# Gathers paced by the landing of the one three back, in a recommendation tower on one core

## What is computed

```python
e = stack([tbl_f[ids[:, f]] for f in range(26)], axis=1)      # (512, 26, 64): the gathers
x = layer_norm(dense_t @ Wd.T, gd, bd)                        # (512, 128)
y = layer_norm(einsum('bnd,ed->bne', e, Ws), gs, bs)          # (512, 26, 128)
y = layer_norm(einsum('bne,pn->bep', y, Wsi), gsi, bsi)       # mixes the 26 features to 32
T = concatenate([x[:, None, :], swapaxes(y, 1, 2)], axis=1)   # (512, 33, 128)
Z = einsum('bnd,bmd->bnm', T, T)                              # pair products of the 33
z = layer_norm(Z[:, TRIL_I, TRIL_J] @ Wl.T, gl, bl)           # 528 -> 512, 384 kept
h = concatenate([z, dense_t], axis=1)
h = relu(h @ W_top1 + b_top1); h = relu(h @ W_top2 + b_top2); out = h @ W_top3
```

## Time and profile before

| | us |
|---|---|
| median of 3 runs | 211.37 (209.83 to 212.67) |
| the profiled execution | 211.83 |
| its span, first to last instruction | 210.0 |

### The profile page before, as it was taken

How to read it: one execution, slowest core, us unless ns; L and a number is a source line. 1 busy time by engine, 2 the same in 40 slices (tenths; PEclk the granted TensorE clock), 3 DMA queues, 4 the chain that set the end, 5 groups by cost and what they waited for, 6 DMA issues and landing times.

```text
span 210.0 us, 4185 instructions
## 1 busy us (share of the span) xinstructions
PE 162.5 (77%) x1644; PEld 105.3 (50%) x1644; DVE 99.3 (47%) x192; ACT 88.5 (42%) x225; POOL 100.0 (48%) x113
## 2 busy tenths in 40 slices
PE   0593888683798795948986878579877969997996
PEld 0332635351355363726554637355555567465574
DVE  2463928635457655553072738260545574661011
ACT  2613235451164664541473436232644535642251
POOL 4777374667474664765546557736173710000000
PEclk9999589999599998596999999958999978999999
DMA  6713314172011144111101243101010630005100
GB/s 160 229 21 79 108 29 112 33 246 53 16 25 18 29 118 76 28 26 21 25 6 30 81 91 53 28 16 27 4 28 13 153 50 3 0 3 138 24 3 0
DMA packets 20260, 11.58 MB, mean 55 GB/s; under 512 B 12945, under 2 KB 17681, under 8 KB 20242
## 3 DMA queue, kind: packets, MB, share of 16 engines
q1 hardware_dynamic: 16226, 7.83, 14.2%
q0 software_dynamic: 3328, 3.41, 8.6%
q10 hardware_dynamic: 688, 0.08, 0.3%
HBM read 9.15 MB, written 2.16 MB: 54 GB/s over the span
## 4 chain that ended last, share of the span: by engine, by line
PE 63%; issue 19%; DVE 10%; DMA 4%; ACT 3%; SPq 0%; ACTq 0%; DVEq 0%
PE proj_ps L474 11%; PE mix_ps L440 10%; PE o_ps L490 8%; PE quad_ps L451 7%; PE dots_ps L465 6%; PE o_turn_ps L403 3%; PE o_turn_ps L528 2%; DVE var_p L881 2%; PE turn_ps L432 2%; PE o_ps L403 2%; DVE feats L905 2%; DVE e_prod L890 2%; DVE var_n L893 2%; PE o_ps L422 2%; PE dots_ps L396 2%
## 5 line engine op out<-in xcount | busy, mean ns | idle before, releaser
L373 POOL DMA_INDIRECT e_rows<-table_dram,rows_sb x104 | 99.1, 953 | 68.1 <-PE dots_ps L465 33.8
L890 DVE TENSOR_TENSOR e_prod<-quad_ps,e_rows 128x384 f32<-128x384 f32 (+1 forms) x16 | 9.5, 591 | 56.6 <-PE quad_ps L451 44.7
L465 PE MATMUL dots_ps<-feats 128*32 128x33 f32 x1024 | 19.1, 203 | 21.2 <-issue 20.8
L474 PE MATMUL proj_ps<-f_sb,proj_w 128*128 128x512 f32 x60 | 32.2, 619 | 1.3 <-DVE feats L905 0.6
L465 PEld LDWEIGHTS dots_ps<-feats 128*32 128x32 f32 x1024 | 14.6, 113 | 36.1 <-issue 35.0
L440 PE MATMUL mix_ps<-mixw_sb,e_unit 128*128 128x192 f32 (+4 forms) x128 | 26.7, 364 | 6.3 <-issue 5.1
L440 PEld LDWEIGHTS mix_ps<-mixw_sb,e_unit 128*128 128x128 f32 x128 | 24.8, 235 | 13.6 <-issue 9.9
L682 ACT COPY f_sb<-mix_ps 64x512 f32<-64x512 f32 x32 | 18.5, 579 | 20.1 <-PE mix_ps L440 16.4
L490 PE MATMUL o_ps<-wl_gained,z_pairs 128*128 128x512 f32 (+1 forms) x40 | 21.2, 664 | 0.5 <-DMA z_pairs<-z_dram 0.5
L451 PEld LDWEIGHTS quad_ps<-gram,e_cols 128*128 128x128 f32 x104 | 13.4, 194 | 16.3 <-issue 11.0
L881 DVE TENSOR_REDUCE var_p<-y_sq 128x16 f32<-128x512 f32 x32 | 20.5, 677 | 1.6 <-ACT y_sq L667 1.6
(11 more groups left out here) (142 smaller groups left out, 176.8 us busy)
## 6 DMA issues: line engine op xcount, KB each, us to landing
z_dram<-z_mine SPq DMA_DIRECT2D x4, 512.0 KB, 3.2
e_rows<-table_dram,rows_sb POOLq DMA_INDIRECT x104
w_sb<-w_dram SPq DMA_DIRECT2D x2, 512.0 KB
wl_sb<-wl_dram SPq DMA_DIRECT2D x2, 512.0 KB
w_sb<-w_dram SPq DMA_DIRECT2D x1, 768.0 KB
dense_sb<-dense_t_dram SPq DMA_DIRECT2D x1, 512.0 KB
wl_sb<-wl_dram SPq DMA_DIRECT2D x1, 256.0 KB
z_pairs<-z_dram SPq DMA_DIRECT2D x4, 64.0 KB, 2.1
```

The costliest lines, as they stand in the source:

```text
L373: pool.indirect_dma_start(out=e_rows[:, chunk, t, D * ab:D * (ab + 1)], out_offset=None, in_=table, in_offset=bass.IndirectOffsetOnAxis(ap ...
L465: mm = pe.matmul(dots_ps[PR * k:PR * (k + 1), (PR + 1) * g:(PR + 1) * (g + 1)], f[:, 2:PR + 2], f[:, 0:PR + 1], start=True, stop=True)
L474: pe.matmul(proj_of(s, ab), proj_w[:], f_sb[:, q % 2, ab, :], start=True, stop=True).then_inc(projected, 1)
L890: dve.tensor_tensor(e_prod[:, 0:2 * nt, :].rearrange("p a d -> p (a d)"), quad_ps[:, 0:P * nt], e_rows[:, chunk, t0:t0 + nt, :].rearrange( ...
```

## The change

The 16 semaphores of the slots are replaced by four, `landed[0]` to `landed[3]`; gather g adds to `landed[g % 4]`. Gather g waits for the landing of gather g - 3. The waits before slots 2 and 3 are gone; from slot 4 on a slot's first gather waits for `dots` of four slots back, as it did. Who reads a slot's landing (`turn`, SyncE's loads) waits on all four semaphores for their share of the gathers up to that slot's last (`rows_landed`). `variance_n` no longer waits for the landing; it waits for `quad`, which comes after `turn`.

```diff
--- before.py
+++ after.py
@@ -104,6 +104,14 @@
         if lo < hi:
             parts.append((t, lo - first_sample(t), lo - q * QB, hi - lo))
     return parts
+
+
+IN_FLIGHT = 3
+
+
+def gathers_up_to(s):
+
+    return sum(2 * tiles_of(slot % QUARTERS)[1] for slot in range(s + 1))
 
 
 
@@ -231,7 +239,7 @@
         ids_in, small_in, mixw_in, dense_in = sem("ids_in"), sem("small_in"), sem("mixw_in"), sem("dense_in")
         w1_in, wl_in, w2_in, out_done = sem("w1_in"), sem("wl_in"), sem("w2_in"), sem("out_done")
         pairs_in, w1_dense_in = sem("pairs_in"), sem("w1_dense_in")
-        gathered = [[sem(f"gathered{chunk}_{q}") for q in range(QUARTERS)] for chunk in range(CHUNKS)]
+        landed = [sem(f"landed{k}") for k in range(IN_FLIGHT + 1)]
         rows_ready = sem("rows_ready")
         consts = sem("consts")
         prep_dve, prep_pe, prep_act = sem("prep_dve"), sem("prep_pe"), sem("prep_act")
@@ -269,6 +277,12 @@
             if not isinstance(count, int) or count > 0:
                 eng.wait_ge(semaphore, count)
 
+        def rows_landed(eng, s):
+
+            number = gathers_up_to(s)
+            for k in range(IN_FLIGHT + 1):
+                eng.wait_ge(landed[k], 16 * ((number - 1 - k) // (IN_FLIGHT + 1) + 1))
+
         def is_last(chunk):
             return isinstance(chunk, int) and chunk == CHUNKS - 1
 
@@ -308,10 +322,10 @@
             sp.dma_start(pairs_sb[:], pairs).then_inc(pairs_in, 16)
 
             for q in range(3):
-                sp.wait_ge(gathered[0][q], 32 * tiles_of(q)[1])
+                rows_landed(sp, q)
                 begin, end = q * KZ // 3, (q + 1) * KZ // 3
                 sp.dma_start(wl_sb[:, begin:end, :], wl[:, begin:end, :]).then_inc(wl_in, 16)
-            sp.wait_ge(gathered[0][3], 32 * tiles_of(3)[1])
+            rows_landed(sp, 3)
             sp.dma_start(w1_sb[:, 0:KU, :], w1[:, 0:KU, :]).then_inc(w1_in, 16)
             sp.dma_start(w2_sb[:], w2).then_inc(w2_in, 16)
 
@@ -356,24 +370,22 @@
             pool.memset(feats[:, :, :, 0], 1.0).then_inc(consts, 1)
             pool.wait_ge(rows_ready, 1)
 
-            def after_round(i):
-                if i >= 2:
-                    pool.wait_ge(dotted, i - 1)
-                elif i >= 0:
-                    pool.wait_ge(mixed, i + 1)
-                    pool.wait_ge(gathered[0][i + 1], 32 * tiles_of(i + 1)[1])
-
-            for chunk in range(CHUNKS):
-                for q in range(QUARTERS):
-                    after_round(chunk * QUARTERS + q - 2)
-                    t0, nt = tiles_of(q)
-                    for t in range(t0, t0 + nt):
-                        for ab in range(2):
-                            col = (chunk * TILES + t) * 2 + ab
-                            pool.indirect_dma_start(
-                                out=e_rows[:, chunk, t, D * ab:D * (ab + 1)], out_offset=None, in_=table,
-                                in_offset=bass.IndirectOffsetOnAxis(ap=rows_sb[:, col:col + 1], axis=0),
-                            ).then_inc(gathered[chunk][q], 16)
+            for s in range(SLOTS):
+                chunk, q = place(s)
+                t0, nt = tiles_of(q)
+                if s >= 4:
+                    pool.wait_ge(dotted, s - 3)
+                for n in range(2 * nt):
+                    g = gathers_up_to(s) - 2 * nt + n
+                    if g >= IN_FLIGHT:
+                        older = g - IN_FLIGHT
+                        pool.wait_ge(landed[older % (IN_FLIGHT + 1)], 16 * (older // (IN_FLIGHT + 1) + 1))
+                    t, ab = t0 + n // 2, n % 2
+                    col = (chunk * TILES + t) * 2 + ab
+                    pool.indirect_dma_start(
+                        out=e_rows[:, chunk, t, D * ab:D * (ab + 1)], out_offset=None, in_=table,
+                        in_offset=bass.IndirectOffsetOnAxis(ap=rows_sb[:, col:col + 1], axis=0),
+                    ).then_inc(landed[g % (IN_FLIGHT + 1)], 16)
 
         @block.tensor
         def _(pe):
@@ -426,7 +438,7 @@
             def turn(s):
                 chunk, q = place(s)
                 t0, nt = tiles_of(q)
-                pe.wait_ge(gathered[chunk][q], 32 * nt)
+                rows_landed(pe, s)
                 wait(pe, cols_ready, s)
                 for t in range(nt):
                     mm = pe.transpose(turn_ps[:, P * t:P * (t + 1)], e_rows[:, chunk, t0 + t, :], eye_sb)
@@ -886,7 +898,6 @@
                 t0, nt = tiles_of(q)
                 dve.wait_ge(quad_done, s + 1)
                 wait(dve, std_ready, s)
-                dve.wait_ge(gathered[chunk][q], 32 * nt)
                 dve.tensor_tensor(e_prod[:, 0:2 * nt, :].rearrange("p a d -> p (a d)"), quad_ps[:, 0:P * nt],
                                   e_rows[:, chunk, t0:t0 + nt, :].rearrange("p t d -> p (t d)"), ALU.mult).then_inc(prod_done, 1)
                 dve.wait_ge(prod_done, s + 1)
```

## The result

The changed kernel takes 222.91 us (median of 4, 218.85 to 224.72) beside 210.6 us (209.75 to 212.67) for the kernel before: 1.045 times as long, 95% interval 1.026 to 1.064. It is slower, where I had forecast 209.5 us and within 2%. The profiled execution took 223.88 us, its span 222.1, against 211.83 and 210.0.

What follows compares the result with a forecast made beforehand. Two chains were taken to bound the kernel, holding each other: a slot's gathers wait for `dots` of four slots back, and `dots` for landings. 211.83 - 1.85 = 210.0 us, 209.5 on the median; 8 in 10 for 206.3 to 213.6.

Steps and rivals of the forecast that it cites:

- The stop has to do with outstanding gathers: TensorE's stops inside `dots`, 20.8 us in all: each lasts until the outstanding gathers have landed.
- another cause: Rival: stops in `dots` don't come from gathers; `dots(0)` keeps its 3.5 us, only the first-slot delay stays: 211.9 us; chance 0.13.
- TensorE waited for neither slot, so this by itself gives nothing: Slots 2 and 3: removing GpSimd's waits lands gathers earlier, but gains TensorE 0 by itself.
- `dots(0)` runs in one piece: First pair products: no gather outstanding, so no stop; 0.8 us long, ending near 40.3 in place of 42.85.
- Steady gathers, 0: Between gathers: the landing three back is seen 1.4 us before it is wanted, so the new wait costs 0.
- costly-wait rival: Landing wait costs in the idle before each gather: 214.3 us at 0.1 us each, 223.9 at 0.30; chance 0.12.
- transposes' waits: Transposing steps wait on four semaphores for one: taken as 0, at most 0.30 us a step, 4.8 us for 16.
- The first slot, 1.7 us later: Start: gather 3 waits for gather 0, starting near 8.75 for 7.09; `dots(0)` starts 0.35 to 0.7 us later.
- Slots 2 and 3, three microseconds earlier: Gathers without the waits before these slots: slot 3 seen landed near 39.45 in place of 42.48.
- 1.85 us: Slot 4's eighth gather seen landed at 52.36 for 54.21, `dots(1)` ending there; the whole kernel gains this.
- The clock: TensorE's stretches at 1.2 GHz: one spared gives 206.5 us (chance 0.15), one added 212.5 (chance 0.05).
- The weight loads: Rival: upper layers' loads stop `dots` as gathers do, holding `dots(0)` to 44.3: 212.9 us; chance 0.05.

Runs made afterwards that it cites:

- e2: The kernel before without its waits before slots 2 and 3 and without any wait for the gather three back: 218.35 us, 1.051 of the kernel before.
- e5: e2 with 24 tiny matmuls (48 matmul records) added behind `quad(0)`: 222.16 us, 1.070 of the kernel before.
- e6: The kernel before with every second group of pair products left out, 32 matmuls in a `dots` for 64: 200.64 us, 0.966.
- e7: The kernel before with only chunk 0 gathered (26 gathers for 104), later chunks computing on its rows: 173.43 us, 0.837.
- e3: The changed kernel with both old waits before slots 2 and 3 put back: 213.92 us, 1.005 of the kernel before (1.023 by medians).
- e13: e2 with 48 long-past semaphore waits of TensorE behind `quad(0)`: 176.71 us, 0.993 of the kernel before, which took 177.55 us beside it.
- e16: e2 with 120 long-past semaphore waits of ScalarE behind its first copy: 177.23 us, 0.996 of the kernel before, which took 177.55 us beside it.
- e18: The kernel before with all of GpSimd's waits between gathers left out: 173.66 us, 0.977 of the kernel before, which took 177.75 us beside it.
- e8: The kernel before with the gathers from slot 4 on dealt more evenly between the `dots`: 205.8 us, 0.989.
- e9: The kernel before with a pause in each slot from slot 4 on, until its first four gathers have landed: 205.56 us, 0.989.
- e4: The kernel before without the wait for `mix` before slots 2 and 3, the landing waits kept: 210.54 us, 1.007 by medians.

## Why the prediction was wrong, point by point

**The stop has to do with outstanding gathers**: right, where the hold is there. e2, e5, e6 and e7 bear it out, and my rival "another cause" is out. I was wrong, though, to write there that the measurement decides on the fetch of instructions: rows 2 show stops without a named end, not a fetch. What I built on it was wrong: I took the stops for a matter of a long burst, one that outgrows what is queued at TensorE, and so for a matter of `dots` alone. It is a count of matmuls, or of something that goes with them, since the gathers began, over whatever step. The trace before had it already. The eight stopped `dots` stop after 38, 39, 33, 34, 37, 25, 27 and 27 of their own matmuls, which tells nothing; counted from the first gather of the string that is outstanding, it is after 56, 57, 57, 58, 56, 55, 61 and 57.

**"TensorE waited for neither slot, so this by itself gives nothing"**: this is the step that failed. True as to data. But the two pauses left short moments with nothing outstanding (2.2 and 1.1 us), and in the strings before them TensorE had done only some 30 and 20 matmuls, less than its allowance. Without them one string ran from 9.22 to 39.8 us, and TensorE stood in it for 11.25 us. I had priced the pauses as a gain of 3.0 us for the landings and nothing for TensorE; e2 puts the loss at 5.1%, 9 to 11 us. The forecast that `dots(0)` runs in one piece came true, but by luck: my sum put its start at 39.45 to 39.8, the trace has it at 53.71, when the last gather had been down for 13.9 us.

**Steady gathers, 0**: half right. The wait itself costs nothing where it is met; 0.30 us idle and 1.25 us from gather to gather stayed, as forecast. But I checked only the undisturbed gather, seen landed 1.4 us early. Some landings come late. Behind gather 3 the trace after has seven idle times over 0.30 us inside slots, 3.7 us above it in all, five of them ended by a landing, where I had one of 0.7. Three of the five stand at the writes of `z`; at the other two the late gather shared its time with a single packet of the instruction queue (123.8 and 147.3 us). With the hold they cost at most some 2% (e3 has them). Without it they are most of the loss. The costly-wait rival had the right sign and the wrong place: not at each gather, but at a few. (Its 0.09 for "slower" holds 0.05 for the transposes' waits that the list of chances leaves out.)

**The first slot, 1.7 us later**: right, a little too small. Gather 3 started at 9.22 (forecast 8.75, upper bound 9.4), SyncE saw slot 0 landed at 17.46 (16.9), TensorE's first transposes started at 17.52 and the copy at 18.19 (17.85).

**Slots 2 and 3, three microseconds earlier**: nearly. SyncE's load came at 40.20 (forecast 39.45). Slot 4's gathers, forecast near 40.6, came at 54.75, behind the late `dots(0)`, and so the 1.85 us that I summed up never came into play; nor was its fourth gather late.

**The clock**: there are seven stretches at 0.50 in place of six, and they take 51.2 us together where they took 34.1, about TensorE's stop above all. Right behind the stop that costs 2.6 us; over the whole span the busy time of the matmuls did not grow. The forecast had it as a rival of 3 us, either way. **The weight loads** stopped nothing: they go out at 40.20, when TensorE comes back.

**What stays open**: what the allowance is, what exactly it counts, and why it is there in some groups of runs and not in others. The supply of instructions is the nearest suspect. The Trainium skill (Runtime: NRT & Kernel Launch, Instruction fetch mechanics) says that prefetch hides it mostly; in the changed kernel not one packet of the instruction queue moved between 29 and 46 us, so it was not a fetch that the trace shows. e13 and e16 were made to settle it and ran where nothing is held. It wasn't tried whether the hold is there in an execution that is not recorded. Nor has e18 run with the hold; I expected over 260 us for it there.

## What to carry to other kernels

A pause of one engine can be what another lives on. Before you take one away, look not only for who waits for its end, but for what becomes possible during it, here a moment with no gather outstanding. A wait for the n-th last transfer is free only if it is met at the slowest landing, not at the usual one; look for it where other transfers are large. And take the kernel before along in each group of runs: here it moved by 30 us by itself, and what was best changed with it (e18 without the hold, e8 and e9 with it).

## What the runs showed of the hardware

With the hold, TensorE does mostly 45 to 65 matmuls (73 in one string of e8), each with its weight load, from the start of a string of gathers, and then one or a few in 0.7 or 1.4 us until the string has landed; 0.5 us without a gather outstanding lifts it (e4). Without the hold, a string leaves TensorE alone: in e13, from gather 26 on, there was no moment with nothing outstanding for 99 us, and TensorE did over 1100 matmuls in it, with 0.1 us idle before the 1024 of all `dots`. A matmul's drawn end can be far too early: `quad(1)` is drawn to 32.19, and its reader started at 41.93. A gather mostly takes 0.94 us of GpSimd (up to 1.36 in the first slot of the kernel before) and 0.30 us to the next, with others outstanding or not, and its last packet mostly ends 2.0 to 2.4 us after its start; beside the weight loads, gather 26 of e9 took 4.5 us.
